# Up-projection blocks all from rounded parts in a ring of four, with the rounding of the score maxima on another engine

## The chip, the cores and the metric

The kernel runs on one core of a Trainium2 chip. The metric is the device time of one execution in microseconds. A core has TensorE (matrix products), VectorE, ScalarE and GpSimd, which run their own streams of instructions in order, and SyncE, which issues DMA transfers. They meet through semaphores.

## The reference

Eight batches of 512 rows with 256 columns pass through two attentions and a mixture of experts. Cut to what matters here:

```python
x = L0_attn_query                                   # (8, 512, 256)
x = x + _layernorm(attn(_layernorm(x)))             # 16 heads, rope, window of 250
# the second part, ffn(src) with src = _layernorm(x):
x = _rmsnorm(src + full_attention(src) @ Wo, norm1_w)
shared = _swiglu(flat @ W_shared_in) @ W_shared_out     # 256 -> 2 x 512 -> 256
h = _swiglu(flat @ W1_shared)                           # 256 -> 2 x 512, for all experts
routed = sum(h @ W2_experts[e] * w[:, e:e + 1] for e in range(8))   # w: two of eight are not zero
out = _rmsnorm(x + shared + routed, norm2_w)
```

## The kernel before

The matrices are tiled to 128 partitions. A batch i is worked on in two bodies, each of them heads (projection, rotation, transposes to the stacks q_t and k_t), then `attention(i, f, e, a)` with a = 0 for the windowed attention and a = 1 for the full one. Beside the first body the previous batch f = i - 1 does its up projection; beside the second body, and beside the heads, its expert outputs; the last of these run in the batch after that (e).

`attention` is a loop over steps m from -28 (LEAD) to 63. At step m TensorE makes the max score unit m + 28 (line 750), VectorE takes its maximum (1229 or 1232), and for m >= 0 TensorE makes the score unit m (777), whose exponentials ScalarE takes (630), GpSimd masks (505, 509) and TensorE weighs (791). Four groups of 16 steps (UNITS) cover 16 heads. Steps below 0 are called the lead here, the others the quiet steps. When the 16 maxima of a group are there, `split_max` rounds them into a high and a low part in m_split (VectorE, 1243 and 1244); TensorE transposes them (`max_rows`, 759, two units later), ScalarE copies the rows, and SyncE places them in q_t by small DMAs (`place_maxima`, 352). The score units of the group wait for those.

The up projection has 2 * NH = 8 blocks of hidden columns, each with a gated half and another half, and two input chunks: 32 products a batch. `HIDDEN_AT` gives the step of each: 16 in the lead, 16 at QUIET, steps 2, 5, 9 and 13 of each group. Blocks 0 to 3 (W_shared_in) multiply rounded parts: high and low weights times high and low rows, three matmuls a product (line 826, weights wup_r, rows xn_hi and xn_lo, which live in the stack buffers). Blocks 4 to 7 (W1_shared) are plain float32 matmuls (line 830, weights wup_s, kept in SBUF), of which each shows as two records. The rounded weights come from DRAM (wup_parts) through wup_r, a ring of RING = 2 blocks, by `load_up` on SyncE. They are made once, by GpSimd in batch 0 (`split_up`), and so are the expert pairs (`split_pair`).

VectorE follows each block with two operations (`gated_half` 1408, `hidden` 1415), two steps after the product that they need. In the last batch the up projection runs alone in `last_hidden`, with six banks in turn, and VectorE does STEPS_AT_LAST = 9 steps of other work (gates, the finish of the batch before) after each block.

Between the transposes of the second source xn and the product after them TensorE runs `unread(st[1], 2)` (line 879), two matmuls that nothing reads, while ScalarE copies the transposed rows. Their results are not used.

What sets the order: each engine's program is written out by hand in these tables of steps, and each runs in order.

## Time and profile before

| | us |
|---|---|
| three runs | 1986.41, 1979.39, 1984.70 |
| median | 1984.7 |
| the profiled execution's own time | 1978.52 |
| its span, first to last instruction | 1976.8 |
| TensorE busy | 1833.7 (93%) |
| VectorE busy | 1345.6 (68%) |
| ScalarE busy | 807.6 (41%) |
| GpSimd busy | 382.1 (19%) |

A busy share says how long an engine had work, over all stages; it doesn't say which engine a stage waits for. Matmuls overlap in the profile, so that a busy TensorE can still have waited a little. In the rows below, PE is TensorE, DVE is VectorE, ACT is ScalarE, POOL is GpSimd, and PEclk is the granted TensorE clock as a share of 2.4 GHz.

### The profile page before, as it was taken

The page shows a single profiled execution, that of the slowest core. Times are in us where ns is not written, and L with a number is a line of the kernel's source. Part 1 is how long each engine was busy: PE and PEld are TensorE (multiplying, and loading weights), DVE is VectorE, ACT ScalarE, POOL GpSimd, SP SyncE. Part 2 cuts the span into 40 slices and gives each one's busy share as a digit, 9 for nine tenths or more (in the row PEclk, how much of TensorE's full clock was granted, in tenths as well). Part 3 has the DMA queues.
Part 4 walks back from the last instruction along what each step waited for, and adds up shares of the span by engine and source line. Part 5 has one row for each costly group of instructions (what it writes and reads, how often), then busy time and mean ns, then how long its engine had stood idle before and what let it go on. Part 6 is the DMA issues. An engine that isn't in the chain of part 4 may idle for free.

```text
span 1976.8 us, 27875 instructions
## 1 busy us (share of the span) xinstructions
PE 1833.7 (93%) x9216; PEld 1022.6 (52%) x9216; DVE 1345.6 (68%) x4116; ACT 807.6 (41%) x1730; POOL 382.1 (19%) x671
## 2 busy tenths in 40 slices
PE   7968899989999999999999999998999999999988
PEld 4343464636555364644637355463645537364466
DVE  6457474775768668685876857677586856868466
ACT  3433535245343634335353353425534363443510
POOL 2336024101231013200251011410123101320010
PEclk8585999999999999999999999899999999999999
DMA  3026002201031100401022010220103110040240
GB/s 110 2 84 236 23 22 87 86 2 54 23 139 44 44 22 13 163 20 48 29 97 87 2 54 23 97 85 2 54 23 139 44 44 23 26 157 1 97 170 11
DMA packets 31295, 123.04 MB, mean 62 GB/s; under 512 B 5424, under 2 KB 18352, under 8 KB 26544
## 3 DMA queue, kind: packets, MB, share of 16 engines
q1 hardware_dynamic: 28624, 105.54, 14.9%
q0 software_dynamic: 2528, 15.73, 2.1%
q8 instruction: 73, 1.20, 0.2%
q14 instruction: 70, 0.57, 0.1%
HBM read 101.33 MB, written 18.87 MB: 61 GB/s over the span
## 4 chain that ended last, share of the span: by engine, by line
PE 74%; DVE 17%; issue 5%; ACT 3%; DMA 1%; POOL 0%; SPq 0%; DVEq 0%; ACTq 0%; POOLq 0%
PE fb L852 12%; PE ot L791 10%; PE sm L750 8%; PE fb L830 6%; DVE negmax L1232 6%; PE st L777 5%; PE fb L826 4%; PE st L718 3%; PE dn L718 3%; PE fb L848 3%; PE st L734 3%; DVE sm L1229 2%; DVE acc L1430 2%; PE sm L777 2%; PE ot L718 2%
## 5 line engine op out<-in xcount | busy, mean ns | idle before, releaser
L630 ACT ACTIVATE probs<-st 128x512 f32<-128x512 f32 (+3 forms) x832 | 395.4, 507 | 388.1 <-PE st L777 384.4
L852 PE MATMUL fb<-w_r,h_r 128*128 128x512 f32 x1344 | 391.5, 418 | 0.0
L750 PE MATMUL sm<-k_t,q_t 48*128 48x512 f32 (+3 forms) x864 | 313.8, 447 | 63.8 <-DVE negmax L1229 31.1
L1232 DVE TENSOR_REDUCE negmax<-sm 128x1 f32<-128x512 f32 x416 | 268.8, 685 | 83.5 <-PE sm L750 83.4
L777 PE MATMUL st<-q_t,k_t 64*128 64x512 f32 (+3 forms) x832 | 298.7, 453 | 22.3 <-ACT probs L630 19.9
L750 PEld LDWEIGHTS sm<-k_t,q_t 48*128 48x128 f32 x864 | 144.5, 195 | 315.3 <-DVE negmax L1229 136.5
L852 PEld LDWEIGHTS fb<-w_r,h_r 128*128 128x128 f32 x1344 | 231.0, 189 | 92.3 <-issue 56.3
L1229 DVE CUSTOM_DVE_ANT_0 sm<-sm,mask_qk 128x384 f32<-128x384 f32 (+1 forms) x448 | 202.1, 469 | 94.6 <-PE sm L750 91.5
L791 PE MATMUL ot<-probs,v_s 128*32 128x512 f32 (+3 forms) x2048 | 252.7, 536 | 2.9 <-POOL probs L505 2.9
L464 POOL TENSOR_TENSOR stack<-rot,stack 128x256 fp32r<-128x256 f32 x64 | 50.0, 782 | 980.7 <-ACT stack L566 980.7
L777 PEld LDWEIGHTS st<-q_t,k_t 64*128 64x128 f32 x832 | 133.6, 193 | 122.4 <-ACT probs L630 88.0
L505 POOL TENSOR_SCALAR_AFFINE_SELECT probs<-probs 128x256 f32<-128x256 f32 x256 | 105.6, 413 | 374.2 <-ACT probs L630 373.6
L1430 DVE SCALAR_TENSOR_TENSOR acc<-fb,gate,acc 128x256 f32<-128x256 f32 x224 | 107.8, 481 | 79.8 <-PE fb L852 74.5
L830 PE MATMUL fb<-xn_t,wup_s 128*128 128x512 f32 x232 | 130.2, 646 | 0.0
L826 PE MATMUL fb<-stack,wup_r 128*128 128x512 f32 x348 | 110.4, 434 | 1.4 <-DMA wup_r<-wup_parts 1.4
L630 ACT ACTIVATE probs<-sm 128x512 f32<-128x512 f32 (+2 forms) x192 | 85.6, 501 | 39.5 <-PE sm L777 39.2
L791 PEld LDWEIGHTS ot<-probs,v_s 128*32 128x32 f32 x2048 | 51.6, 110 | 78.2 <-issue 41.5
L566 ACT ACTIVATE stack<-rot 128x512 fp32r<-128x512 f32 x128 | 73.7, 624 | 43.1 <-DVE rot L1213 42.2
L734 PE MATMUL st<-ident_r,stack 128*128 128x128 f32 x704 | 85.1, 256 | 5.3 <-DVE q_t L1218 3.6
L1249 DVE RECIPROCAL den<-dn 128x16 f32<-128x16 f32 x64 | 16.2, 254 | 106.5 <-PE dn L803 106.3
L566 ACT ACTIVATE xn_t<-dn 128x512 f32<-128x512 f32 x40 | 23.9, 598 | 158.0 <-PE dn L713 158.0
L734 PEld LDWEIGHTS st<-ident_r,stack 128*128 128x128 f32 x704 | 69.1, 141 | 21.2 <-issue 8.9
(214 smaller groups left out, 2589.9 us busy)
## 6 DMA issues: line engine op xcount, KB each, us to landing
w_r<-w_parts SPq DMA_DIRECT2D x30, 2048.0 KB, 8.0
wup_r<-wup_parts SPq DMA_DIRECT2D x32, 512.0 KB, 4.0
w_parts<-w_r POOLq DMA_DIRECT2D x4, 2048.0 KB, 9.4
x_s<-in_L_attn_query SPq DMA_DIRECT2D x8, 512.0 KB, 4.7
q_t<-rot_b SPq DMA_DIRECT2D x256, 4.0 KB
x_kept<-o_s SPq DMA_DIRECT2D x8, 512.0 KB, 3.0
h_s<-in_L_ffn_W_experts POOLq DMA_DIRECT2D x8, 512.0 KB, 5.3
xa<-x_kept SPq DMA_DIRECT2D x8, 512.0 KB, 3.3
```

The lines of the kernel that those rows point to most:

```text
L630: nc.scalar.activation(probs[:, n % PSLOTS, 0:hi - lo], score_bank(m)[:, 0:hi - lo], ACT.Exp, scale=float(D) ** -0.5).then_inc(s_ex, 1)
L718: last = mm(dst, src_t[:, c, t * P:(t + 1) * P], w[:, c, :], start=(c == 0), stop=(c == NC - 1))
L734: last = nc.tensor.transpose(stack_bank(a, t, k)[:, b * P:(b + 1) * P].bitcast(F32R), stack[:, t % 2, pr:pr + 2, :].rearrange("p h s -> p ...
L750: mm(max_bank(w, a)[:, 0:hi - lo], q_t[r:r + MROW, b, t * P:(t + 1) * P], k_t[r:r + MROW, b, lo:hi], start=True, stop=True).then_inc(s_sm, 1)
L777: mm(score_bank(w)[:, 0:hi - lo], k_t[r:r + SK, b, j * P:(j + 1) * P], q_t[r:r + SK, b, lo:hi], start=True, stop=True).then_inc(s_st, 1)
L791: last = mm(ot[VW * c:VW * (c + 1), lo:hi], v_s[:, j, g * GH + c, :], probs[:, n % PSLOTS, 0:hi - lo], start=(j == 0), stop=(j == NT - 1), ...
L826: product = mm(bank[:, :], wup_r[:, n % RING, w, half, c, :], (xn_hi, xn_lo)[x][:, c], start=(c == 0 and k == 0), stop=(c == NC - 1 and k ...
L830: product = mm(bank[:, :], wup_s[:, c, col:col + P], xn_t[:, c, :], start=(c == 0), stop=(c == NC - 1))
L852: last = mm(fb[q % 2][:, :], h_r[:, h, m, rows], w2_r[:, k % 2, w, m, :], start=(m == 0 and n == 0), stop=(m == NH - 1 and n == 2))
L1229: return v.tensor_tensor_reduce(scores, scores, mask_qk[:, BACK * P - (hi - lo):BACK * P], -1.0, -MASKED, ALU.add, ALU.min, negmax[:, g % ...
L1232: return v.tensor_reduce(negmax[:, g % 2, n // GH, c:c + 1], max_bank(g * UNITS + n, a)[:, 0:hi - lo], AX.X, ALU.max, negate=True).then_in ...
L1430: add = v.scalar_tensor_tensor(acc[:, t, :], fb[q % 2][:, (e % 2) * E:(e % 2 + 1) * E], gate[:, t, e:e + 1], acc[:, t, :], ALU.mult, ALU.add)
```

## The change

1. Blocks 4 to 7 take the path of blocks 0 to 3: their weights are split into rounded parts too (a second `split_up`, before the expert pairs), stored in wup_parts, and loaded block by block. wup_s and its load are gone. Each product is now three matmuls on rounded parts (line 845 of the changed kernel).
2. RING is 4. In a batch SyncE loads four blocks after the residual and blocks 4 and 5, 6, 7 between the groups of `place_maxima`.
3. QUIET has five steps a group (2, 4, 6, 9, 13), so the lead has 12 products. QUIET_OUT starts at step 3 in every group, and the slices of expert outputs in the second body's lead end a step earlier.
4. For all batches but the first, `split_max` runs on GpSimd. VectorE gets a wait for it before the first maximum of groups 2 and 3.
5. The `unread` after the transposes of xn becomes slice 0 of expert output 7, which stood in the heads of the second body.
6. STEPS_AT_LAST is 9, 9, 4, 4, 4, 4 for the blocks of the last batch, and 9 beside the shared outputs as before.

```diff
-QUIET = [g * UNITS + n for g in range(NGR) for n in (2, 5, 9, 13)]
-QUIET_OUT = [g * UNITS + n for g in range(NGR) for n in ((2, 8, 12) if g else (3, 8, 12))]
+QUIET = [g * UNITS + n for g in range(NGR) for n in (2, 4, 6, 9, 13)]
+QUIET_OUT = [g * UNITS + n for g in range(NGR) for n in (3, 8, 12)]
...
-OUT_AT = [-LEAD] + spread(len(OUT_BESIDE) * NH - len(QUIET_OUT) - 1, 1 - LEAD, 1) + QUIET_OUT
+OUT_AT = [-LEAD] + spread(len(OUT_BESIDE) * NH - len(QUIET_OUT) - 1, 1 - LEAD, 0) + QUIET_OUT
-RING = 2
-STEPS_AT_LAST, STEPS_BESIDE_LAST = 9, 9
+RING = 4
+STEPS_AT_LAST, STEPS_BESIDE_LAST = (9, 9, 4, 4, 4, 4), 9
...
# SyncE, place_maxima, after the four DMAs of group g
+                    if f is not None:
+                        for n in ((4, 5), (6,), (7,), ())[g]:
+                            load_up(f, n)
...
# SyncE, load_up
-                if n >= RING:
+                if n >= RING or not isinstance(f, int) or f > 0:
                     sp.wait_ge(s_ub, f * N_UB + n - RING + 1)
-                elif f > 0:
-                    sp.wait_ge(s_ub, (f - 1) * N_UB + NH - RING + n + 1)
...
# GpSimd
+            def split_max(i, a, gr):
+
+                count = (i - 1) * N_MS + a * NGR + gr + 1
+                pool.wait_ge(s_mx, i * N_MX + (a * NGR + gr + 1) * UNITS)
+                if gr >= 2:
+                    pool.wait_ge(s_mp, i * N_MP + a * NGR + gr - 1)
+                m = negmax[:, gr % 2].rearrange("p t (b h) -> p h b t", b=2)
+                hi = m_split[:, gr % 2, :, 0]
+                lo = m_split[:, gr % 2, :, 1]
+                g.tensor_copy(hi, m).then_inc(s_mh, 1)
+                pool.wait_ge(s_mh, count)
+                g.tensor_tensor(lo, m, hi.bitcast(F32), ALU.subtract).then_inc(s_ms, 1)
...
+                    if f is not None and m % UNITS == 2 and m // UNITS + 1 < NGR:
+                        split_max(i, 0, m // UNITS + 1)
...
# TensorE, after the transposes of xn
-                    unread(st[1], 2)
+                    expert_out(f, 7, 0)
...
# VectorE, attention
-                        take_max(i, a, *divmod(m + LEAD, UNITS))
+                        gr, n = divmod(m + LEAD, UNITS)
+                        if f is not None and gr >= 2 and n == 0:
+
+                            dve.wait_ge(s_ms, i * N_MS + a * NGR + gr - 1)
+                        take_max(i, a, gr, n)
...
-                    if (m + LEAD) % UNITS == UNITS - 1 and m + LEAD < ALL:
+                    if f is None and (m + LEAD) % UNITS == UNITS - 1 and m + LEAD < ALL:
                         split_max(i, a, (m + LEAD) // UNITS)
```

TensorE in the first quiet group, steps 2 to 6, before. L830 is a plain up product, L750 a max score unit, L777 a score unit, L759 the transpose of the maxima:

```order
L830 MATMUL fb<-xn_t,wup_s 128x512
L750 MATMUL sm<-k_t,q_t 128x384
L777 MATMUL st<-q_t,k_t 128x384
L750 MATMUL sm<-k_t,q_t 128x128
L777 MATMUL st<-q_t,k_t 128x384
L750 MATMUL sm<-k_t,q_t 128x128
L777 MATMUL st<-q_t,k_t 128x384
L830 MATMUL fb<-xn_t,wup_s 128x512
L750 MATMUL sm<-k_t,q_t 128x128
L777 MATMUL st<-q_t,k_t 128x384
L759 MATMUL dn<-ident,m_split 32x128
```

And with the change, from the same product on (L845 is the product, L774 the max unit, L801 the score unit, L783 the transpose):

```order
L845 MATMUL fb<-stack,wup_r 128x512 x3
L774 MATMUL sm<-k_t,q_t 128x384
L801 MATMUL st<-q_t,k_t 128x384
L774 MATMUL sm<-k_t,q_t 128x128
L801 MATMUL st<-q_t,k_t 128x384
L845 MATMUL fb<-stack,wup_r 128x512 x3
L774 MATMUL sm<-k_t,q_t 128x128
L801 MATMUL st<-q_t,k_t 128x384
L774 MATMUL sm<-k_t,q_t 128x128
L801 MATMUL st<-q_t,k_t 128x384
L783 MATMUL dn<-ident,m_split 32x128
L845 MATMUL fb<-stack,wup_r 128x512 x3
```

The product that followed step 5's units now stands after step 4's, and one more stands after the transpose in step 6.

GpSimd at the start of the first body's masks of batch 1, before (L537 makes the low rows, L505 and L509 mask):

```order
L537 TENSOR_TENSOR stack<-xn_t,stack 128x32x16 [waits expert_rows_high_made,stack_transposes_done]
L537 TENSOR_TENSOR stack<-xn_t,stack 128x32x16 [waits expert_rows_high_made]
L505 AFFINE_SELECT probs<-probs 128x2x128 [waits exps_done]
L509 AFFINE_SELECT probs<-probs 128x2x134
L505 AFFINE_SELECT probs<-probs 128x2x128 [waits exps_done]
L509 AFFINE_SELECT probs<-probs 128x2x134
```

And with the change (L556 makes the low rows, L502 and L504 round the maxima, L515 and L519 mask):

```order
L556 TENSOR_TENSOR stack<-xn_t,stack 128x32x16 [waits expert_rows_high_made,stack_transposes_done]
L556 TENSOR_TENSOR stack<-xn_t,stack 128x32x16 [waits expert_rows_high_made]
L502 CAST m_split<-negmax 128x2x8 [waits max_taken]
L504 TENSOR_TENSOR m_split<-negmax,m_split 128x2x8 [waits max_high_made_by_pool]
L515 AFFINE_SELECT probs<-probs 128x2x128 [waits exps_done]
L519 AFFINE_SELECT probs<-probs 128x2x134
L515 AFFINE_SELECT probs<-probs 128x2x128 [waits exps_done]
L519 AFFINE_SELECT probs<-probs 128x2x134
L502 CAST m_split<-negmax 128x2x8 [waits max_taken]
L504 TENSOR_TENSOR m_split<-negmax,m_split 128x2x8 [waits max_high_made_by_pool]
```

The rounding of group 0 stands ahead of the first mask, that of group 1 behind the masks of steps 0 to 3.

## Rows read from the trace of the kernel before

**Rows 1.** Windows: us; PE, PEld, DVE, ACT, POOL busy; PEclk; DMA share; GB/s.
```profile
936.40:1044.70 108.30, 103.83 (x557) 58.24 (x556) 81.84 (x302) 47.33 (x114) 35.79 (x70) 1.00 0.17 60
1044.70:1168.80 124.10, 117.38 (x591) 64.41 (x590) 84.34 (x208) 52.78 (x101) 6.17 (x8) 1.00 0.15 52
1168.80:1282.80 114.00, 109.63 (x557) 60.10 (x556) 81.87 (x302) 47.42 (x114) 35.76 (x70) 0.94 0.16 57
...
972.00:977.00 5.00, 5.00 (x26) 3.39 (x25) 4.06 (x15) 0.60 (x1) 0.00 (x0) 1.00 0.27 103
```
**Rows 2.** Chain of waits, end of the first body's lead: start us, us, what.
```profile
981.29 0.21 DVE st L1229
...
987.10 0.44 PE sm L750
```
**Rows 3.** Chain of waits: up products of both kinds in the first body.
```profile
971.29 0.93 PE fb L826 x3
...
972.93 1.67 PE fb L826 x6
...
987.54 1.06 PE fb L830 x2
...
1031.61 0.86 PE fb L830 x2
```
**Rows 4.** Timelines of PE and DVE: start, us, instruction, idle before and releaser.
```profile
989.84 0.32 PE L750 MATMUL sm<-k_t,q_t 48*128 48x128 f32 x1 [0.69 <-DVE negmax L1229]
...
989.82 0.32 DVE L1243 CAST m_split<-negmax 128x16 fp32r<-128x16 f32 x1
...
990.42 0.15 DVE L1384 TENSOR_TENSOR gprob<-gprob,esum 128x4 f32<-128x4 f32 x1
...
1108.49 0.50 PE L750 MATMUL sm<-k_t,q_t 48*128 48x512 f32 x1 [1.43 <-DVE negmax L1232]
```
**Rows 5.** Chain of waits through the second body's heads and lead.
```profile
1059.07 0.86 PE st L879 x4
...
1064.98 3.00 PE fb L852 x12
...
1088.73 4.79 DVE negmax L1232 x8
...
1093.86 0.49 DVE acc L1430
```
**Rows 6.** GpSimd's small operations (timeline), and all casts of the maxima (min/median/max ns).
```profile
57.20 0.20 POOL L509 TENSOR_SCALAR_AFFINE_SELECT probs<-probs 128x12 f32<-128x12 f32 x1
...
132.18 0.72 POOL L464 TENSOR_TENSOR stack<-rot,stack 128x256 fp32r<-128x256 f32 x1 [22.93 <-ACT stack L566]
...
L1243 DVE CAST m_split<-negmax x64: 174/176/980, 41.8 to 1841.8; 128x16 fp32r<-128x16 f32 x64
```
**Rows 7.** Tail: one block on the chain, then the timeline of TensorE.
```profile
1882.69 3.02 PE st L826 x12
...
1891.87 3.17 PE L826 MATMUL fb<-stack,wup_r 128*128 128x512 f32 x12 [1.45 <-DMA wup_r<-wup_parts]
...
1908.10 3.60 PE L830 MATMUL sm<-xn_t,wup_s 128*128 128x512 f32 x8
1915.24 8.86 PE L848 MATMUL fb<-wso_s,h_s 128*128 128x256 f32 x32 [3.55 <-DVE sg L1451]
```
**Rows 8.** GpSimd in batch 0: low parts of the up weights, and its last store.
```profile
103.47 4.66 POOL L526 TENSOR_TENSOR h_r<-h_s,h_r 128x1024 fp32r<-128x1024 f32 x2
...
186.09 0.59 POOL L489 DMA_DIRECT2D w_parts<-w_r  x1 [0.30 <-POOL w_r L485]
```
**Rows 9.** From the page: a hidden operation of VectorE, and the loads of the ring.
```profile
L1415 DVE SCALAR_TENSOR_TENSOR sg<-sg,fb 128x512 f32<-128x512 f32 x28 | 19.2, 686 | 20.6 <-PE fb L830 20.2
...
wup_r<-wup_parts SPq DMA_DIRECT2D x32, 512.0 KB, 4.0
```
**Rows 10.** Window in the quiet steps of batch 5, columns as in rows 1.
```profile
1230.00:1245.00 15.00, 13.84 (x59) 5.42 (x59) 8.77 (x36) 6.42 (x16) 5.33 (x12) 0.61 0.01 3
```

More of the change, by code:

```diff
@@ L227, in build @@
         s_ms, N_MS = sem("max_split"), 2 * NGR
+        s_mh = sem("max_high_made_by_pool")
         s_mp, N_MP = sem("max_transposed"), 2 * NGR
@@ L269, in build @@
         s_wup = sem("up_weights_stored")
-        s_wu, N_WU = [sem(f"up_weights_loaded{k}") for k in range(RING)], 16 * NH // RING
-        wup_parts = nc.dram_tensor("wup_parts", (NH, P, 2, 2, NC, P), F32, kind="Internal").ap()
+        s_wu, N_WU = [sem(f"up_weights_loaded{k}") for k in range(RING)], 16 * 2 * NH // RING
+        wup_parts = nc.dram_tensor("wup_parts", (2 * NH, P, 2, 2, NC, P), F32, kind="Internal").ap()
         w2_parts = nc.dram_tensor("w2_parts", (PAIRS, P, 2, NH, 2 * E), F32, kind="Internal").ap()
@@ L386, in batch @@
                     x1_from_dram(e)
-                if f is not None:
-                    for n in range(RING, NH):
-                        load_up(f, n)
-                place_maxima(i, 0)
+                place_maxima(i, 0, f)
                 if f is not None:
@@ L409, in _ @@
             batch(0, None, None, True)
-            sp.wait_ge(s_wup, 16)
+            sp.wait_ge(s_wup, 32)
             for n in range(RING):
@@ L420, in _ @@
             load_pair(B - 1, 1, B - 2)
-            for n in range(RING, NH):
+            for n in range(RING, 2 * NH):
                 load_up(B - 1, n)
@@ L515, in mask_probs, with load_up_raw, split_up @@
                                 hidden_low(f, k)
-            def split_up():
-                pool.wait_ge(s_wur, 16)
+            def load_up_raw(u):
+                if u > 0:
+                    pool.wait_ge(s_wul, NC * u)
+                g.dma_start(wup_raw, (w_si, w1)[u].rearrange("(c p) n -> p c n", p=P)).then_inc(s_wur, 16)
+            def split_up(u):
+                pool.wait_ge(s_wur, 16 * (u + 1))
+                if u > 0:
+                    pool.wait_ge(s_wup, 16 * u)
                 for c in range(NC):
@@ L539, in rows_low @@
                                     ALU.subtract).then_inc(s_xl, 1)
-            g.dma_start(wup_raw, w_si.rearrange("(c p) n -> p c n", p=P)).then_inc(s_wur, 16)
+            load_up_raw(0)
             low_parts(0, 0)
             mask_probs(0, None)
-            split_up()
+            split_up(0)
+            load_up_raw(1)
             low_parts(0, 1)
+            split_up(1)
             load_raw(0)
@@ L555, in _ @@
                 rows_low(i - 1, i * N_SP + 16)
+                split_max(i, 0, 0)
                 mask_probs(i, i - 1)
                 low_parts(i, 1)
+                for gr in range(NGR):
+                    split_max(i, 1, gr)
             rows_low(B - 1, B * N_SP)
@@ L817, in hidden @@
                     pe.wait_ge(s_xl, f * N_XL + c + 1)
-                if n < NH and s % 4 == 0:
+                if s % 4 == 0:
                     pe.wait_ge(s_wu[n % RING], f * N_WU + 16 * (n // RING + 1))
-                up_product(fb[half], f, n, half, c)
-            def up_product(bank, f, n, half, c):
-                if n < NH:
-                    for k, (w, x) in enumerate(((0, 0), (0, 1), (1, 0))):
-                        product = mm(bank[:, :], wup_r[:, n % RING, w, half, c, :], (xn_hi, xn_lo)[x][:, c],
-                                     start=(c == 0 and k == 0), stop=(c == NC - 1 and k == 2))
-                else:
-                    col = half * HID + (n - NH) * P
-                    product = mm(bank[:, :], wup_s[:, c, col:col + P], xn_t[:, c, :], start=(c == 0), stop=(c == NC - 1))
+                for k, (w, x) in enumerate(((0, 0), (0, 1), (1, 0))):
+                    product = mm(fb[half][:, :], wup_r[:, n % RING, w, half, c, :], (xn_hi, xn_lo)[x][:, c],
+                                 start=(c == 0 and k == 0), stop=(c == NC - 1 and k == 2))
                 if c == NC - 1:
@@ L1046, in last_hidden @@
                             pe.wait_ge(s_xl, f * N_XL + c + 1)
-                        if half == 0 and c == 0 and n < NH:
+                        if half == 0 and c == 0:
                             pe.wait_ge(s_wu[n % RING], f * N_WU + 16 * (n // RING + 1))
-                        up_product(hidden_banks[n % 3][half], f, n, half, c)
+                        for k, (w, x) in enumerate(((0, 0), (0, 1), (1, 0))):
+                            product = mm(hidden_banks[n % 3][half][:, :], wup_r[:, n % RING, w, half, c, :],
+                                         (xn_hi, xn_lo)[x][:, c], start=(c == 0 and k == 0), stop=(c == NC - 1 and k == 2))
+                    product.then_inc((s_up, s_ub)[half], 1)
             def last_expert_out(t, k):
@@ L1611, in _ @@
                 if n < 2 * NH - 2:
-                    for _ in range(STEPS_AT_LAST):
+                    for _ in range(STEPS_AT_LAST[n]):
                         next(others, None)
@@ L1615, in _ @@
                 last_shared_out(q)
-                for _ in range(STEPS_AT_LAST):
+                for _ in range(STEPS_AT_LAST[0]):
                     next(others, None)
```

16 lines of the change are left out of this document (7 added, 9 removed).

## The prediction

> **What bounds the kernel now.** I read the busy time by stage first [rows 1]. A batch repeats every 232.4 us in two bodies, the first attention (936.4 to 1044.7) and the second (1044.7 to 1168.8). TensorE is busy for 103.8 of 108.3 us and for 117.4 of 124.1 us; VectorE for 81.8 and 84.3. TensorE is the bound on average, but it idles 4.5 + 6.7 us a batch, and the reader should look for those. Then the chain of waits [rows 2]: up to 981.2 it is one unbroken run on TensorE, and from there to the end of the lead (987.1) it hops between VectorE and TensorE. So the lead has a TensorE part and a VectorE part. Among the quiet steps TensorE stands 0.69 us before the sixth step of a group (step 5, counted from 0), waiting for a maximum [rows 4]. In the second body the lead's chain is nearly all maxima on VectorE [rows 5]. The last batch's tail is a third stage, with its own waits [rows 7].
>
> **Dearer or cheaper products.** A first-half product of the up projection is three single-pass matmuls: 1.67 us for two, 0.83 each (0.93 where it starts after a maximum). A second-half product is two records of 1.06 us together, 0.86 at the least [rows 3]. The change makes all 16 second-half products of a batch of the first kind. Price: 16 x (1.06 - 0.93) = 2.1 us of TensorE work less a batch; the ends are no gain (0.86 against 0.83) and 16 x 0.23 = 3.7. The Trainium skill ("FP8 and Floating Point Precision", TensorE Precision Notes) says true FP32 takes four passes of the array. By that rule, as an estimate, four passes against three would save a quarter of the time; the rows show an eighth to a fifth, so the rows decide.
>
> **The lead of the first body.** It drops from 16 to 12 products. Before step -10, where the chain is TensorE's, ten become seven: 3 x 0.93 = 2.8 us. After it the chain is VectorE's, 5.9 us [rows 2]; one operation of 0.69 of the up projection's [rows 9] leaves it. That makes 3.5 at best. But VectorE is already busy for 4.06 of 5.0 us at 972 to 977 [rows 1], so squeezing TensorE makes the maxima late sooner. Walking the steps with 0.93 a product, 0.3 to 0.66 a maximum and 0.68 a gated step, I get the end of the lead 2.4 us earlier. Ends: 1.2 and 3.5.
>
> **The quiet steps of the first body.** 16 products become 20. TensorE work: 4 x 0.93 more, 16 x 0.13 less, so +1.6 us. Against it stands idle time that the new places fill: the product that stood at step 5 is now at step 4 and another at 6, so the 0.69 us wait before the maximum of step 5 [rows 4] is covered in groups 0 and 1, and about 0.4 of a like wait in group 2: -1.8. The hidden product of VectorE at the end of group 0 moves to step 11, out of a stretch that VectorE bounds: up to -0.6, of which I take half. At the end GpSimd gets a 1.4 us subtraction at step 58 instead of 52, ahead of the last two masks; TensorE already waits there for a mask: +0.3. Sum +1.6 - 1.8 - 0.3 + 0.3 = -0.2. First body: -2.4 - 0.2, and I shave it to **-2.2** for waits that I can't see; ends -0.5 and -3.5.
>
> **The maxima's rounding moves from VectorE to GpSimd.** Eight pairs of small operations a batch. In the quiet stage the cast starts at 989.82 and VectorE's next work at 990.42, 0.65 us with the gap ahead; in the second body VectorE ends its maxima at 1093.52 (1088.73 + 4.79) and goes on at 1093.86; back-to-back operations overlap by about 0.1, which makes 0.43 us [rows 4, 5]. In the first body three of them sit beside the waits counted above, and I count nothing more. In the second body two lie on the chain: at 1093.6 (chain all VectorE) and at 1106.5, behind which TensorE stands 1.43 us [rows 4]. 2 x 0.43 = 0.9; a third (1122.7) may give 0.3: **-1.2**, ends 0 and -1.7. What is new is a wait of TensorE's transpose of the maxima for GpSimd, and everything on TensorE is queued behind it. No row shows this operation on GpSimd. Nearest rows: 0.20 us for 128x12 and 0.72 for 128x256 [rows 6]; I take 0.2 each, 0.5 for the pair with its semaphore. The transpose comes two maxima after the last of its group, at least 0.9 us later; in the quiet steps three steps, over 3 us. It is hidden; uncovered it costs its excess over that. GpSimd is in order: its masks wait behind the pair by no more than 0.5 us and were 8 slots ahead. VectorE's new wait (group two's first maximum on the pair of two groups before) is met a group earlier.
>
> GpSimd's operations and VectorE's can hold each other up: the cast of a maximum takes 174 ns at best, 335 among the masks, 980 at the worst [rows 6]. The Trainium skill ("SBUF — State Buffer", Who interferes with whom) calls the shared port pair an exclusive lock, where the loser blocks for the whole instruction; the trace agrees in direction. It speaks against more small work on GpSimd. By the rows the price is at most 16 pairs of 0.2 us, and what VectorE's own casts paid among the masks (0.65 against 0.43) goes. I count zero.
>
> **The filler.** Between the transposes of the second source and its projection TensorE runs a filler of 0.86 us, then later a group of 12 matmuls in 3.0 us that VectorE's next rotation waits behind [rows 5]. Now three of those 12 (0.75) stand in the filler's place. They need one output read by VectorE, which starts right after the second source is ready (TensorE's transposes of it start at 0.9 us before the filler) and takes 1.0 us, so the bank is free within 0.2 us of TensorE getting there (1059.07). The filler's time goes, the later group shrinks: **-0.8**; ends 0 and -0.9. The second body's three quiet slices move by one step: zero, ends +0.5 and -1.5. Second body: **-2.0**, ends +0.5 and -3.5 (-1 likely at least).
>
> **The ring and the loads.** 1 MB a batch becomes 2 MB after the residual and 2 MB inside the first body, 0.5 MB at a time at 4.0 us each [rows 9]; it used to be 1 MB and 1 MB. SyncE issues blocks 4 and 5 behind the score rows of group 0 (step -9), needed at 13 and 25; blocks 6 and 7 at 7 and 23, needed at 38 and 52. A step is 0.8 us, so each has 12 us or more. DMA is busy for 17% of the stage [rows 1]. Hidden; uncovered, 4 us each. In the start GpSimd gets about 8 us more (4.66 for the low parts, 2 for the high ones, gaps and an issue) before the expert weights; they are done at 186 and now near 195, an estimate,, needed only in batch 1 [rows 8]. Zero, ends -3 and +3.
>
> **The tail.** Before, TensorE waits 1.45 us for block 2 until 1891.87, runs two blocks of 3.02 and four of 3.43 (1908.10 is the last one's start: 2 x 3.02 + 3 x 3.43 = 16.3), and then waits 3.55 us for VectorE until 1915.24 [rows 7]. The ring holds four blocks already; block 4's load takes the place of block 2's and lands by 1891.7, five us before its use. So block 2 starts at 1890.4 and six blocks of 3.02 end at 1908.5. VectorE now does four side steps a block, not nine, 1.3 + 1.7 us against 3.0; its last product adds 0.75: 1909.3. **-5.9**; ends -4 and -6.5. The 19 side steps left over run beside the shared outputs, 8.9 us of TensorE.
>
> **The sum.** Seven batches have this work: 7 x (2.2 + 2.0) = 29.4, and 5.9: 35.3 us. The profiled execution took 1978.5 us (span 1976.8) and is the shortest of those shown; the median is 1984.7. I subtract from the median: **1949 us**. From the profile it would be 1943. The difference may be the clock: in this execution TensorE fell from 2.4 to 1.2 GHz once, in batch 5 (0.61 of it granted at 1230 to 1245), in steps with waits for VectorE, and that body took 114.0 instead of 108.3 us [rows 1, 10]. The medians may hold more such falls.
>
> **Rivals.**
> A, VectorE takes over: the lead gives 1.2, the quiet steps cost 0.7, the second body gives 1.0. 7 x 1.5 + 5.9 = 16.4: 1968. For it: VectorE has little room after 976. Chance 0.17.
> B, the clock: denser quiet steps remove the fall, and all parts come near their upper ends: 7 x 6 + 6 + 5.7 = 54: 1931. Chance 0.13.
> C, the other way with the clock: the fall comes in every batch, since steps 14 to 17 are as empty as before. 6 x 5.7 = 34 us takes all of it: 1983, no change. Against it: six of seven batches have none. Also here: the ring hides nothing that cost time and the products save nothing. Chance 0.10.
> D, slower: GpSimd hands the rounded maxima over late, and TensorE stands before the transpose in each first-body group. Behind a mask (0.8) and a held-up subtraction (1.4) that is 2.2 us beyond its slack, three times in seven batches, 46 us: 1985 + 46 - 35 = 1996. It decides from the point where the pair ends later than step 6 of a group. Against it: over 3 us of slack. Chance 0.05.
>
> **How the numbers follow.** The forecast (1935 to 1965) has 0.55. A measurement tells 0.5% from no change, that is 1975 to 1995. Faster by more: the forecast, A and B, 0.85. Same: C, 0.10. Slower: D, 0.05. The range 1928 to 1972 takes in the forecast, A's and most of B's times, and leaves out about 0.2.
>
> **What would show it.** The batch period near 228 us; TensorE busy 3 us a batch less; the first body near 106, the second near 122; no wait over 0.3 us at step 5; no release of the transpose by GpSimd; no wait for up blocks; the shared outputs starting 38 us after the last attention's end, not 43.6. A period above 231, or the transpose waiting for GpSimd, would make the prediction wrong.

## The result, and the profile after

The changed kernel took **1998.2 us** (median of six runs, 1990.5 to 2028.6) against 1985.0 us for the kernel before on the same chip (six runs, 1973.4 to 1990.0). The ratio is 1.0059, with a 95% interval of 1.0033 to 1.0085: 0.6% slower, where 1949 us and faster was forecast. (The run of 2028.6 us, over 1.5% above the fastest, is left out of the ratio.) The profiled execution took 2001.8 us (span 2000.0) at a mean granted clock of 0.940; that of before took 1978.5 us (span 1976.8) at 0.962.

I cut both spans at the end of the last exponential of each attention. A first body is then its heads, its lead and its quiet steps, all counted from the end of the second body before it. The columns of the window rows are those of [rows 1]; the last three are the granted clock, the DMA share and GB/s. First the changed kernel: batch 0, the seven first bodies in order, and the tail.

```profile
0.00:231.70 231.70, 186.11 (x798) 91.51 (x798) 128.84 (x380) 95.29 (x204) 90.38 (x125) 0.68 0.31 111
231.70:343.50 111.80, 105.25 (x574) 62.99 (x570) 65.68 (x246) 46.96 (x113) 33.27 (x75) 0.97 0.16 58
467.70:582.30 114.60, 109.65 (x572) 65.17 (x566) 79.69 (x293) 46.92 (x113) 34.99 (x75) 0.93 0.18 65
706.60:821.30 114.70, 109.75 (x572) 65.16 (x566) 79.94 (x293) 46.96 (x113) 35.05 (x75) 0.93 0.18 65
945.50:1060.60 115.10, 109.67 (x572) 65.09 (x566) 80.00 (x293) 47.05 (x114) 35.05 (x75) 0.93 0.17 65
1184.80:1292.80 108.00, 102.73 (x572) 60.69 (x566) 79.60 (x293) 46.98 (x114) 35.03 (x75) 1.00 0.19 69
1417.00:1529.10 112.10, 107.01 (x572) 63.30 (x566) 79.86 (x293) 46.99 (x114) 35.05 (x75) 0.95 0.18 67
1653.20:1768.00 114.80, 109.83 (x572) 64.73 (x566) 80.02 (x293) 46.96 (x114) 34.98 (x75) 0.93 0.17 65
1892.20:2000.00 107.80, 96.13 (x428) 75.98 (x422) 68.76 (x234) 11.07 (x22) 7.65 (x6) 0.97 0.30 115
```

The same cuts in the kernel before: batch 0, an ordinary first body, the one with the fall of the clock that [rows 10] showed, and the tail.

```profile
0.00:226.30 226.30, 178.27 (x798) 86.75 (x798) 129.69 (x380) 95.07 (x204) 82.21 (x119) 0.72 0.27 99
462.30:570.80 108.50, 104.35 (x558) 58.17 (x554) 81.63 (x301) 46.72 (x114) 34.11 (x68) 1.00 0.15 55
1159.60:1273.40 113.80, 110.14 (x558) 60.01 (x554) 81.62 (x301) 46.78 (x114) 34.11 (x68) 0.94 0.15 52
1862.50:1976.80 114.30, 99.79 (x412) 74.11 (x406) 70.57 (x234) 11.37 (x21) 7.62 (x6) 0.97 0.26 99
```

Between the two spans lie 23.2 us. Batch 0 gave +5.4, the seven first bodies +24.6 (791.1 against 766.5), the seven second bodies -0.3 (869.5 against 869.8), the tail -6.5. So nearly all of the loss is in the first bodies, and six of seven there have a granted clock below 1. (In five of them, batches 2 to 4, 6 and 7, a fall begins in the lead, 41.7 to 44.7 us into the body; in batch 1 it begins at the lead's end and lies in the quiet steps.) One, from 1184.8, has full clock throughout and takes 108.0 us, 0.4 less than before. That row is the important one: **two things went wrong, not one.** The clock cost some 33 us (the six others against 108.0, of batch 1's against 110, since it took 110.6 before with full clock; an estimate from these rows), and even with full clock the change brings next to nothing outside the tail.

Cut finer, with the lead's end at the first exponential. First the stretches of an undisturbed batch of before (heads and lead, then quiet steps; first body, then second).

```profile
927.20:985.70 58.50, 58.19 (x289) 39.69 (x284) 41.86 (x145) 18.00 (x36) 9.41 (x10) 1.00 0.08 28
985.70:1035.60 49.90, 46.16 (x270) 18.45 (x272) 39.66 (x157) 28.66 (x78) 24.70 (x58) 1.00 0.23 84
1035.60:1103.70 68.10, 65.73 (x322) 44.05 (x316) 49.97 (x125) 16.86 (x34) 7.84 (x10) 1.00 0.20 72
1103.70:1159.60 55.90, 51.13 (x275) 20.45 (x276) 34.70 (x86) 36.59 (x70) 0.00 (x0) 1.00 0.11 39
```

And the changed kernel: a lead with the fall, then the undisturbed batch.

```profile
706.60:770.60 64.00, 62.21 (x277) 42.11 (x272) 41.33 (x146) 17.56 (x35) 9.84 (x12) 0.87 0.07 25
...
1184.80:1242.00 57.20, 55.09 (x277) 37.50 (x271) 40.89 (x145) 17.50 (x35) 9.83 (x12) 1.00 0.08 28
1242.00:1292.80 50.80, 47.65 (x296) 23.19 (x296) 38.71 (x151) 29.48 (x79) 25.20 (x63) 1.00 0.31 116
1292.80:1360.30 67.50, 64.86 (x317) 43.49 (x314) 49.47 (x122) 16.87 (x33) 9.02 (x14) 1.00 0.22 79
1360.30:1417.00 56.70, 50.99 (x275) 20.25 (x278) 34.13 (x81) 36.83 (x70) 1.28 (x6) 1.00 0.11 39
```

At full clock the lead gives 1.3 us, the quiet steps cost 0.9, the second body's lead gives 0.6 and its quiet steps cost 0.8. With the fall the first stretch takes 64.0 us where it takes 57.2. Where does the fall lie? Here are two stretches of the body that starts at 706.6.

```profile
743.30:748.30 5.00, 4.49 (x19) 2.52 (x18) 3.41 (x16) 0.60 (x1) 2.20 (x2) 1.00 0.00 0
748.30:753.30 5.00, 4.83 (x13) 3.23 (x14) 2.62 (x10) 0.00 (x0) 0.00 (x0) 0.50 0.01 3
```

The clock is at 0.50 (1.2 GHz) from 748.3 to 765.4. The timeline of TensorE at its start shows what stood there (start, duration, operation, and in brackets the idle time before it with what ended it).

```profile
746.77 0.65 PE L845 MATMUL fb<-stack,wup_r 128*128 128x512 f32 x2
747.36 0.44 PE L774 MATMUL sm<-k_t,q_t 48*128 48x256 f32 x2
748.47 0.68 PE L774 MATMUL sm<-k_t,q_t 48*128 48x384 f32 x1 [0.68 <-DVE negmax L1248]
749.08 1.02 PE L742 MATMUL dn<-wgate_s,xn_t 128*128 128x10 f32 x4
749.96 1.63 PE L845 MATMUL fb<-stack,wup_r 128*128 128x512 f32 x3
```

L845 is the up product (826 and 830 before), L774 the product for a maximum. TensorE waits 0.68 us for VectorE's maximum, and within this wait the clock goes down; a product then takes 1.63 us instead of the 0.93 of [rows 3]. Ahead of it stand stack transposes of 128 columns, products with 48 rows and with 10 columns, and a few full products. The undisturbed body has the same 0.68 us wait at the same place, so the wait alone does not bring the fall. The Trainium skill ("TensorE: Matmul & The Clock Gate", HAM oscillation) ties such falls to stretches without matmuls. The rows go further than the page: here the longest pause just before the fall was 0.68 us, and TensorE was busy for 4.49 of the last 5.0 us.

The waits of TensorE in the undisturbed first body (us in total, times, longest):

```profile
PE sm L774 <- DVE negmax L1248: 2.4, 6, 0.8
PE ot L815 <- POOL probs L515: 1.2, 2, 0.7
PE dn L783 <- POOL m_split L504: 1.0, 1, 1.0
```

The second of the two waits for masks, at step 50:

```profile
1283.03 0.41 PE L815 MATMUL ot<-probs,v_s 128*32 128x128 f32 x4 [0.74 <-POOL probs L515]
```

The waits for maxima were 3.3 us a batch before, all in the quiet steps, as in [rows 4]. Two thirds of what is left of them stands in the lead now, and two kinds are new: the weighing (L815) waits for GpSimd's masks, and the transpose of the maxima (L783) for GpSimd's rounding. In the second body's quiet steps one wait is new too:

```profile
1408.35 0.66 PE L827 MATMUL dn<-ident,o_t 128*128 128x128 f32 x4 [0.94 <-ACT o_t L590]
1408.76 0.95 PE L868 MATMUL fb<-w_r,h_r 128*128 128x512 f32 x3
```

TensorE waits 0.94 us for ScalarE's copy of the outputs before it transposes them. In the kernel before, the same two stood the other way round, and the slice of an expert output covered ScalarE:

```profile
1150.02 0.96 PE L852 MATMUL fb<-w_r,h_r 128*128 128x512 f32 x3
1151.03 0.66 PE L803 MATMUL dn<-ident,o_t 128*128 128x128 f32 x4
```

The tail did what was forecast. Where [rows 7] had six blocks with side steps and a 3.55 us wait until 1915.24, 52.7 us after the last exponential, the shared outputs now start 46.4 us after it:

```profile
1928.77 3.10 PE L1066 MATMUL fb<-stack,wup_r 128*128 128x512 f32 x12
...
1938.57 2.64 PE L864 MATMUL fb<-wso_s,h_s 128*128 128x256 f32 x11 [0.85 <-DVE sg L1474]
```

### The profile page after: what moved, and what is told of

It reads as the page before. It is cut to its first block, busy times and chain, and to the rows that moved or that the text cites. A ratio compares the mean times of both kernels' runs of the same rounds, so it can differ in the third digit from the quotient of the medians.

```text
span 2000.0 us, 28159 instructions
## 1 busy us (share of the span) xinstructions
PE 1847.0 (92%) x9316; PEld 1061.1 (53%) x9316; DVE 1323.3 (66%) x4004; ACT 811.2 (41%) x1730; POOL 413.6 (21%) x789
## 4 chain that ended last, share of the span: by engine, by line
PE 71%; DVE 15%; issue 6%; ACT 4%; POOL 2%; DMA 1%; SPq 0%; ACTq 0%; DVEq 0%; POOLq 0%
PE fb L868 12%; PE ot L815 10%; PE fb L845 8%; PE sm L774 8%; DVE negmax L1251 6%; PE st L801 4%; PE dn L742 3%; PE st L742 3%; PE st L758 3%; PE fb L864 3%; DVE acc L1453 2%; PE ot L742 2%; PE dn L827 2%; ACT probs L654 2%; PE sm L801 1%
## 5 line engine op out<-in xcount | busy, mean ns | idle before, releaser
L774 PE MATMUL sm<-k_t,q_t 48*128 48x512 f32 (+3 forms) x864 | 313.3, 455 | 49.6 <-DVE negmax L1248 24.0
L801 PE MATMUL st<-q_t,k_t 64*128 64x512 f32 (+3 forms) x832 | 297.4, 456 | 21.7 <-ACT probs L654 19.9
L774 PEld LDWEIGHTS sm<-k_t,q_t 48*128 48x128 f32 x864 | 143.3, 198 | 272.9 <-DVE negmax L1248 115.3
L868 PEld LDWEIGHTS fb<-w_r,h_r 128*128 128x128 f32 x1344 | 230.1, 188 | 85.6 <-issue 49.9
L815 PE MATMUL ot<-probs,v_s 128*32 128x512 f32 (+3 forms) x2048 | 258.2, 538 | 13.8 <-POOL probs L515 13.8
L845 PE MATMUL fb<-stack,wup_r 128*128 128x512 f32 x672 | 244.3, 476 | 0.0
L801 PEld LDWEIGHTS st<-q_t,k_t 64*128 64x128 f32 x832 | 131.4, 193 | 126.2 <-ACT probs L654 90.1
L515 POOL TENSOR_SCALAR_AFFINE_SELECT probs<-probs 128x256 f32<-128x256 f32 x256 | 108.8, 427 | 306.1 <-ACT probs L654 305.8
L1453 DVE SCALAR_TENSOR_TENSOR acc<-fb,gate,acc 128x256 f32<-128x256 f32 x224 | 107.8, 481 | 88.4 <-PE fb L868 83.1
L845 PEld LDWEIGHTS fb<-stack,wup_r 128*128 128x128 f32 x672 | 122.1, 210 | 42.1 <-issue 23.9
L502 POOL CAST m_split<-negmax 128x16 fp32r<-128x16 f32 x56 | 11.4, 204 | 486.6 <-DVE negmax L1251 403.1
L815 PEld LDWEIGHTS ot<-probs,v_s 128*32 128x32 f32 x2048 | 51.9, 110 | 96.6 <-issue 46.4
```

What stands on the lines that cost most here:

```text
L515: last = g.affine_select(out=late, in_=late, compare_op=ALU.is_ge, fill=0.0, base=0, pattern=[[0, 2], [1, P]], channel_multiplier=-1)
L774: mm(max_bank(w, a)[:, 0:hi - lo], q_t[r:r + MROW, b, t * P:(t + 1) * P], k_t[r:r + MROW, b, lo:hi], start=True, stop=True).then_inc(s_sm, 1)
L801: mm(score_bank(w)[:, 0:hi - lo], k_t[r:r + SK, b, j * P:(j + 1) * P], q_t[r:r + SK, b, lo:hi], start=True, stop=True).then_inc(s_st, 1)
L815: last = mm(ot[VW * c:VW * (c + 1), lo:hi], v_s[:, j, g * GH + c, :], probs[:, n % PSLOTS, 0:hi - lo], start=(j == 0), stop=(j == NT - 1), ...
L845: product = mm(fb[half][:, :], wup_r[:, n % RING, w, half, c, :], (xn_hi, xn_lo)[x][:, c], start=(c == 0 and k == 0), stop=(c == NC - 1 an ...
L868: last = mm(fb[q % 2][:, :], h_r[:, h, m, rows], w2_r[:, k % 2, w, m, :], start=(m == 0 and n == 0), stop=(m == NH - 1 and n == 2))
```

## The experiments

**Theories.** L: the lead of 12 products is too thin (TensorE has too little work in it), and that brings the fall of the clock near its end. G: GpSimd's late rounding makes holes that bring it. P: the cheaper products, of three matmuls on rounded parts, bring it.

**1. Four quiet steps in the changed kernel (q4).**

```
-QUIET = [g * UNITS + n for g in range(NGR) for n in (2, 4, 6, 9, 13)]
+QUIET = [g * UNITS + n for g in range(NGR) for n in (2, 5, 9, 13)]
```

> The changed kernel with four quiet steps a group (2, 5, 9, 13) in the first body, so 16 products in the lead as before; all else as changed. Theory L (the thinner lead): in the changed kernel the granted clock fell to 1.2 GHz in six of seven first bodies, at the end of a lead that has 12 products and more waits for VectorE. L expects at most one fall in seven bodies here, first bodies near 107 us (108.3 less about one for the cheaper products), a time of 1965 to 1977. Theory G (GpSimd's late rounding makes the holes) and theory P (the three-pass products themselves bring the fall) both expect that the falls stay: first bodies near 115, a time of 1993 to 2000.

It took 1979.3 us (ratio to before 0.999, 0.996 to 1.002). From batch 2 on no lead has a fall; it takes 58.4 to 58.6 us. But falls remain in the quiet steps: five of these six bodies have one or two, 3.4 to 27.3 us long, and they take 108.3 to 116.5 us. The sixth, without one:

```profile
1399.30:1457.70 58.40, 58.13 (x289) 39.73 (x284) 41.48 (x144) 18.00 (x36) 9.83 (x12) 1.00 0.08 28
1457.70:1506.40 48.70, 44.54 (x286) 21.47 (x288) 38.59 (x151) 28.74 (x78) 26.08 (x64) 1.00 0.30 108
```

So L holds for the lead, and five steps were a loss against four even without the clock: 48.7 + 58.4 = 107.1 against 108.0. TensorE's wait for GpSimd's rounding shrinks from 1.0 to 0.3 us in the undisturbed body, and the two waits of its quiet steps for masks are gone, so these too came from the fifth step. L's "at most one fall" was wrong, and with it its 1965 to 1977 us.

**2. The first body's rounding back on VectorE (s1).**

```
-                        if f is not None and gr >= 2 and n == 0:
+                        if f is not None and a == 1 and gr >= 2 and n == 0:
...
-                    if f is None and (m + LEAD) % UNITS == UNITS - 1 and m + LEAD < ALL:
+                    if (f is None or a == 0) and (m + LEAD) % UNITS == UNITS - 1 and m + LEAD < ALL:
```

(GpSimd's calls of `split_max(i, 0, ...)` are taken out.)

> The changed kernel with the rounding of the maxima of the first body back on VectorE (that of the second body stays on GpSimd). Theory G: the waits of TensorE for GpSimd at the transpose and at the weighing (2.9 us a batch in the changed kernel's undisturbed body) go, and with these holes the falls of the clock: first bodies near 106, a time of 1950 to 1965. Theories L and P: the falls stay in most bodies; the waits for GpSimd shrink by 1 to 2 us a batch, VectorE has 0.4 us more in three places: first bodies near 114, a time of 1985 to 1996.

It took 2012.0 us (ratio 1.014, 1.009 to 1.019). The falls stay in all six leads from batch 2 on, the quiet steps take 50.3 us where they have full clock (50.7 in the changed kernel), and the waits of the weighing for masks stay at 1.2 us a batch. G falls. It ran slower than the changed kernel, in each of its four executions (2002.9 to 2014.3 us). In the profiled one that goes with six disturbed leads against five and with a clock below 1 in the quiet steps of five of the seven bodies; why there are more isn't shown.

**3. Only the rounded up blocks, the ring and the tail (prod).** This is the kernel before with these three.

```
-RING = 2
+RING = 4
...
-STEPS_AT_LAST, STEPS_BESIDE_LAST = 9, 9
+STEPS_AT_LAST, STEPS_BESIDE_LAST = (9, 9, 4, 4, 4, 4), 9
...
+                for k, (w, x) in enumerate(((0, 0), (0, 1), (1, 0))):
+                    product = mm(fb[half][:, :], wup_r[:, n % RING, w, half, c, :], (xn_hi, xn_lo)[x][:, c],
+                                 start=(c == 0 and k == 0), stop=(c == NC - 1 and k == 2))
```

> The kernel before with the rounded up blocks in a ring of four, its load places, and the tail with nine and then four side steps, and nothing else: four quiet steps, filler, rounding on VectorE as before. Theory P: three-pass products bring the falls, first bodies near 114 and a time of 1990 or more. Theories L and G: at most one fall; 16 products at 0.13 us less are 2 us a batch where TensorE is the bound, and 6 to 7 us of tail: 1963 to 1975. If the products' price is hidden, 1978.

It took 1978.7 us (ratio 0.997, 0.995 to 1.000). The tail takes 107.8 us, the same 6.5 less as in the changed kernel. The leads stay at 58.5. The quiet steps of a first body tell more:

```profile
769.70:819.50 49.80, 46.20 (x286) 22.65 (x288) 40.64 (x158) 28.70 (x78) 24.98 (x58) 0.97 0.29 107
```

The clock is 0.97 there, in each first body from batch 3 on: half of the clock for 3.4 us, some 20 us into the quiet steps, where the kernel before had 1.00 in six of seven bodies. (Batch 1 has a fall of 27.3 us in its quiet steps and batch 2 one of 6.8.) The cheaper products should have saved 2.1 us and the stage is 0.1 to 0.2 shorter than 49.9. No fall in the leads: P doesn't explain those. A weaker P would explain the dip; no run takes the products apart from their loads and the ring.

**4. Five quiet steps in the kernel before (b5).** The diff of experiment 1 the other way, in the kernel before.

> The kernel before with five quiet steps a group (2, 4, 6, 9, 13) and so 12 products in the lead, and nothing else. Theory L: the falls come in five or more of seven first bodies, first bodies near 114, a time of 2005 to 2020. Theories G and P: the falls stay away, and the time is 1980 to 1990.

It took 2032.4 us (ratio 1.026, 1.020 to 1.031), slower than anything that L gave. One first body, its lead and its quiet steps:

```profile
716.40:780.60 64.20, 62.22 (x277) 41.66 (x271) 41.79 (x148) 17.52 (x36) 9.40 (x10) 0.86 0.08 26
780.60:834.40 53.80, 51.66 (x280) 21.23 (x280) 40.67 (x153) 29.29 (x79) 23.16 (x57) 0.94 0.23 90
```

A long fall (13.7 to 27.3 us) begins in the lead in four of the six bodies from batch 2 on, one of 3.4 us in the fifth, and in the sixth the fall begins just before the lead ends; all that with nothing of GpSimd's rounding and none of the new products in the kernel. Where the clock is full the quiet steps take 51.9 to 52.0 us, 2.1 more than before, the lead gives 1.1, and the second body's lead takes 68.5 where it took 68.0. So this one edit costs 1.5 us a batch at full clock, and bodies with long falls take 5 to 9 us more. Its quiet steps have the two waits for masks too (1.1 us), with the rounding on VectorE. L is confirmed, and P and G are out as the cause of the falls in the lead.

**5. Fillers in the lead (fill).**

```
-                            gate_logits(f, LOGITS_AT.index(m), 1 if e is None else 0)
+                            gate_logits(f, LOGITS_AT.index(m), 2)
```

> The changed kernel with two 256-column fillers of TensorE (0.86 us a pair, results unread) at each of the four steps of the lead of the first body at which the gate's logits are made, 3.4 us of filling in all, about what the four products that left the lead took. Theory L (the lead is too thin, whatever fills it): the 17 us at 1.2 GHz near the end of the lead go in at least five of seven bodies; lead and heads stage of the first body come down from 63.9 to 58 or 59 us (57.2 undisturbed, plus what of the fillers VectorE doesn't cover); a time of 1970 to 1982. Rival: the fall is tied to the waits for VectorE's maxima in the lead or to GpSimd's small operations and stays: 1998 to 2012.

```profile
704.30:765.20 60.90, 58.79 (x293) 40.60 (x287) 41.12 (x146) 17.52 (x35) 9.81 (x12) 0.99 0.08 25
765.20:819.40 54.20, 51.13 (x298) 25.14 (x296) 38.75 (x148) 29.44 (x79) 25.16 (x63) 0.91 0.29 110
1180.90:1241.60 60.70, 58.59 (x293) 40.58 (x288) 40.90 (x145) 17.52 (x35) 9.81 (x12) 1.00 0.08 27
```

The long falls in the lead are gone: fillers whose results nobody reads do it, with the waits for maxima still there (1.7 us a batch). Batch 1 says the same of every kernel here: there `gate_logits` runs one such filler at each of these steps already (the `1 if e is None` of the line above), and the changed kernel, s1, b5 and qout have no fall over 3.4 us at that place in it. The time is 2003.1 us all the same, not the 1970 to 1982 of L (ratio 1.012, 1.007 to 1.017). The fillers' 3.4 us lie wholly on the path (60.7 against 57.2), so my 58 to 59 was wrong, and in four of seven bodies a fall of 3.4 to 10.2 us came later instead, almost wholly in the quiet steps (clock 0.91 to 0.97).

**6. The second body's quiet slices at their old steps (qout).**

```
-QUIET_OUT = [g * UNITS + n for g in range(NGR) for n in (3, 8, 12)]
+QUIET_OUT = [g * UNITS + n for g in range(NGR) for n in ((2, 8, 12) if g else (3, 8, 12))]
```

> The changed kernel with the quiet slices of the second body at their old steps (2, 8, 12 in groups one to three). In the changed kernel TensorE waits 0.94 us for ScalarE's copy of the outputs at step 50 of the second body, and this stage takes 56.8 us where it took 55.9. If the moved slices are the cause, the wait goes and the stage takes 55.0 to 55.9. If the rounding on GpSimd or the slice in the filler's place is the cause, it stays at 56.8.

```profile
1600.20:1656.20 56.00, 51.75 (x276) 20.60 (x278) 34.16 (x81) 36.76 (x70) 1.27 (x6) 1.00 0.11 39
```

The wait is gone and the stage is back at 55.9 to 56.0 us, in all seven batches. The moved slice cost 0.8 us a batch. (Its time is 2005.6 us from two runs, ratio 1.013, 1.007 to 1.020. The profiled one has falls in five leads from batch 2 on, as the changed kernel, but longer ones, up to 30.7 us; in the first bodies nothing was changed.)

**7. GpSimd's subtractions later (late).**

```
+LOW_AT = (30, 48, 62, 62)
...
-                            if min(HIDDEN_AT[4 * (NH + k) + 3] + HIGH_LAG, ALL - 1) // 2 * 2 == m:
+                            if LOW_AT[k] == m:
```

(The old expression gives 30, 44, 58 and 62.)

> The changed kernel with two of GpSimd's four 1.3 us subtractions for the rounded hidden blocks moved behind masks of which TensorE has no need at once (from step 44 to 48 and from 58 to 62). Theory: TensorE's waits of 0.74 us at the weighing of step 50 and of 0.80 us at the end of the first body come from these subtractions ahead of its masks. Then both go or fall under 0.35: the undisturbed quiet stage takes 49.9 to 50.2 us where it takes 50.7, and the second body's lead 67.0 where it takes 67.5. Rival: they come from the rounding of the maxima on GpSimd or from the masks' own 0.4 us each; then both stay.

```profile
527.30:577.20 49.90, 47.48 (x300) 23.42 (x300) 38.15 (x151) 29.35 (x79) 25.04 (x63) 1.00 0.30 111
577.20:644.00 66.80, 64.67 (x317) 43.30 (x311) 49.45 (x122) 16.84 (x33) 9.47 (x13) 1.00 0.23 86
```

These are the first body's quiet steps and the second body's lead, at full clock. TensorE's wait for a mask at step 50 is gone, and the one behind the end of the first body is down from 0.80 to 0.33: 0.9 us less in the quiet steps, 0.7 in the second body's lead. (One run, 1992.0 us, with long falls in three leads and falls of 3.4 us in two.) In the changed kernel GpSimd's row reads as follows; the mask that TensorE needs stands behind the 1.27 us subtraction.

```profile
1280.97 0.41 POOL L515 TENSOR_SCALAR_AFFINE_SELECT probs<-probs 128x256 f32<-128x256 f32 x1 [0.29 <-ACT probs L654]
1281.35 1.27 POOL L490 TENSOR_TENSOR h_r<-sg,h_r 128x512 fp32r<-128x512 f32 x1
1282.57 0.85 POOL L515 TENSOR_SCALAR_AFFINE_SELECT probs<-probs 128x256 f32<-128x256 f32 x2
```

**8. The kernel before a second time (again).**

> The kernel before, unchanged, a second time. Its first profile had one fall of the clock in seven first bodies (13.7 us long) and 226.3 us up to the end of batch 0. If falls are rare in it, there is again at most one, and the period stays at 232.4 us; the time up to the end of batch 0 shows how far that alone varies with the clock (the changed kernel took 231.7).

One run, 1978.3 us. Batch 0 took 224.7 us, and no first body from batch 2 on has a fall (108.4 to 108.5 each), but some second bodies do (128.3 us in batch 2). Batch 0 varies with the execution: the kernel before, this repetition and b5, which have one program for it, took 226.3, 224.7 and 232.8 us, and nine profiles with the changed kernel's batch 0 took 224.7 to 236.2, all at a granted clock of 0.65 to 0.72. So the 5.4 us of the startup needs no cause in the change; that it has none isn't shown.

**9. Covered and uncovered fillers among the quiet steps (keep).** To prod, two fillers of 0.43 us a group.

```
+KEEP_AT = (4, 12)
...
+                        if m >= 0 and m % UNITS in KEEP_AT:
+                            keep(f, *divmod(m, UNITS))
```

`keep` waits until the bank's last product is read and makes one unread product of 256 columns.

> The kernel before with rounded up blocks, ring of four and the shorter tail, as in run prod, and two fillers of 0.43 us in each group of the first body's quiet steps (after steps 4 and 12), where TensorE waits 0.35 to 0.70 us for a maximum. Theory P2 (the cheaper products thin out the quiet steps, and the clock takes the gain back in a dip of 3.4 to 6.8 us in each body): the dips go, the quiet stage takes 48.6 to 49.4 us where prod has 49.7, a time of 1968 to 1975. Rival: the products' saving is hidden behind VectorE's maxima anyway; the stage stays at 49.7 or grows with the fillers to 51: 1979 to 1990.

```profile
769.80:819.70 49.90, 48.50 (x302) 24.11 (x304) 39.49 (x157) 28.68 (x78) 24.86 (x58) 1.00 0.30 109
```

The dip is gone in five of the six bodies from batch 2 on, and TensorE's waits for maxima fell from 3.1 to 1.2 us a batch; but eight fillers cost about what they bring: the stage takes 49.9 us, not the 48.6 to 49.4 of P2, and the kernel 1983.0 us (ratio 1.001, 0.998 to 1.003).

**10 and 11. The repaired change (best, best2).** The changed kernel with four quiet steps (experiment 1), the old slices (6) and fillers: eight in best, and in best2 only the four that stand where TensorE waits anyway.

```
+KEEP_AT = (4, 20, 28, 36)
...
+                        if m in KEEP_AT:
+                            keep(f, *divmod(m, UNITS))
```

> The changed kernel with four quiet steps a group in the first body (16 products in the lead), the old quiet slices of the second body, and two fillers of 0.43 us in each group of the first body's quiet steps. If the clock and the moved slices are what took the gain: no fall over 3.4 us from batch 2 on, first bodies near 107.2, second bodies near 122.7, a time of 1955 to 1966. If GpSimd's rounding has a price of its own, or the fillers are not covered: first bodies near 109, 1970 to 1980.

> Run best with four fillers in the first body's quiet steps instead of eight, each (after steps 4, 20, 28, 36) where the trace of q4 has TensorE waiting 0.35 to 0.70 us for a maximum. If covered fillers are enough to hold the clock: quiet stage 48.8 to 49.2 us where best has 50.0 (period 230 against 231.2), no fall over 3.4 us from batch 2 on, a time of 1957 to 1965. If the clock wants the others too: falls as in q4 (up to 13.7 us in half of the bodies), 1970 to 1980.

best took 1968.5 us (ratio 0.993, 0.990 to 0.996), between the two ranges expected: no first body from batch 2 on has a fall, but its quiet steps take 50.0 us. **best2 took 1957.2 us: ratio 0.985, 0.981 to 0.990**, faster than both kernels. Its batch:

```profile
927.20:985.60 58.40, 58.03 (x289) 39.56 (x283) 41.55 (x143) 17.99 (x36) 9.83 (x12) 1.00 0.08 28
985.60:1034.10 48.50, 47.18 (x297) 22.87 (x296) 38.68 (x152) 28.71 (x78) 26.11 (x64) 1.00 0.30 110
1034.10:1100.90 66.80, 64.65 (x317) 43.30 (x309) 49.41 (x122) 16.80 (x32) 8.28 (x12) 1.00 0.25 88
1100.90:1156.90 56.00, 51.76 (x275) 20.54 (x278) 34.16 (x81) 36.83 (x70) 1.28 (x6) 1.00 0.11 39
```

A period of 229.7 us against 232.4, with full clock in all twelve bodies from batch 2 on. Four covered fillers hold the clock as well as eight do and leave the quiet steps 1.5 us shorter. Here at last the cheaper products can be seen: 48.4 us a stage where the kernel before has 49.9. The fillers don't make this gain, since the body of q4 with full clock and without them took 48.7; but no run puts fillers into the kernel before, so that the products alone make it is argued, not shown.

**12. best2 with the first body's rounding on VectorE (best2s).**

> Run best2 with the rounding of the first body's maxima back on VectorE (that of the second body stays on GpSimd). Theory S: in the first body GpSimd's rounding is worth nothing where VectorE has room, or costs its waits of the transpose (0.16 us a batch in best2): quiet stage within 0.3 us of 48.4, time 1952 to 1962. Rival: it takes 0.43 us off VectorE's chain in each of the three groups of the quiet stage, and they come back: quiet stage 49.2 to 49.7, time 1962 to 1968.

1959.9 us (ratio 0.987, 0.983 to 0.991), quiet steps 48.3 to 48.6 us, as in best2. The difference from best2 is within the noise: in the first body it does not matter which engine rounds the maxima.

## Why the prediction was wrong, point by point

Per batch, at full clock, in us (the whole run for the tail):

| step of the prediction | forecast | measured | where |
|---|---|---|---|
| lead of the first body | -2.4 | -1.3 | changed kernel, undisturbed body |
| quiet steps | -0.2 | +0.9 | the same |
| second body | -2.0 | +0.2 | the same |
| clock | none | +2 to +7 in six of seven first bodies | changed kernel; cause by b5, q4, fill |
| tail | -5.9 | -6.5 | changed kernel, prod |
| batch 0 | 0 | +5.4 | varies by 8 without the change |

**The clock** was the main failure: some 33 us of the changed kernel's time, where the sum had nothing. The forecast kept the fall of one body in seven out of the sum, and rival B even had the denser quiet steps remove it. I looked at where the one fall of before lay (quiet steps) and asked only what the change does there. The change takes four products out of the lead, and I counted that as pure gain. Rival C (a fall in every batch, 1983 us) was nearest, but placed it at steps 14 to 17 and let the other gains stand. The long falls began in the lead, but for batch 1's: b5 brings them into the kernel before by this edit alone, and q4 and fill take them out of the changed one's leads. Falls in the quiet steps, which q4 keeps and which are longer there than in prod, have no cause shown.

**The lead.** "Walking the steps ... 2.4 us earlier" failed on its own warning: new waits of 1.6 us for VectorE's maxima, two of them 0.68 and 0.81. The undisturbed body also shows what these waits leave: the measured 1.3 is near the lower end that I gave, 1.2.

**The quiet steps.** In the sum +1.6 - 1.8 - 0.3 + 0.3 the failed term is the last, "GpSimd gets a 1.4 us subtraction at step 58: +0.3". Moving such subtractions (late) gave back 0.9 in the quiet steps and 0.7 in the second body's lead, so it was 1.6. I had looked at the last one only; the one at step 44 also stood ahead of a mask that TensorE needed next. With both out of the way the stage takes 49.9 us, as before, where the other terms sum to -0.5; TensorE's wait of 1.0 us for the rounded maximum (below) is still in it.

**The cheaper products.** The 2.1 us was about right as work (0.13 apiece), but it is seen only where the clock stays up: prod shows 0.1 to 0.2, q4's one undisturbed body 1.2, best2 1.5 (with fillers that are covered). In prod a dip of 3.4 us at half clock went with them.

**The second body.** The lead's part was right where no other edit spoils it: 66.8 us in q4 and best2 against 68.0 is -1.2, as much as the 0.8 of the filler and the 0.43 of one rounding (no run takes the two apart). The other roundings (0.43 and 0.3) brought nothing: the wait of 1.43 us in [rows 4] became two of 0.47 and 0.27, yet with the old slices the quiet steps take 55.9 us as before; where the rest went isn't shown. The failed step is "The second body's three quiet slices move by one step: zero, ends +0.5": it was +0.8, since a slice had hidden ScalarE's copy of the outputs. And 0.7 came over from the first body, through GpSimd's late mask (late).

**GpSimd's rounding.** Rival D named the transpose as its place. It did wait, 1.0 to 1.4 us a batch from batch 2 on in the changed kernel, since the pair came behind two masks and took 0.8 us with its gap (my 0.5), and up to 0.3 with four quiet steps. So "hidden" was wrong by a microsecond, D's 46 us by far more. best2s shows that in the first body the move buys nothing.

**Signs.** Two of the prediction's own signs of being wrong came: a period above 231 us (108.0 + 124.2 = 232.2 even with full clock) and the transpose waiting for GpSimd.

**Right:** the tail (a little more than forecast), the loads (no wait for an up block; a load took 5.2 us in the middle instead of the 4.0 of [rows 9], and was hidden), and the place of the first body's old waits.

## What to carry to other kernels

Work that moves off one stretch of TensorE must be checked on the stretch that it leaves: here four full products fewer in a lead of small transposes, short products and waits of 0.7 us halved its clock for 10 to 27 us. Unread fillers at four steps where TensorE waited anyway cost nothing that the stage shows (48.4 us against 48.7) and went with full clock; in the lead, where TensorE didn't wait, they cost their whole time. So read the waits first and place fillers one by one. When slices of work are shifted by "only one step", look for the copy on another engine that the slice had been hiding.

## What the runs showed that I had not expected

- TensorE's clock fell to 1.2 GHz with TensorE busy for 4.49 of 5.0 us and no pause over 0.68 us; the same instructions in another batch of the same execution kept 2.4 GHz.
- Batch 0, at a granted clock of about 0.7, moves the whole by up to 11 us between profiles with the same startup (224.7 to 236.2 us), which is why experiments on this kernel are better read by stage at full clock than by their total.
- Filling the lead didn't free the body of falls: in fill, leads with full clock were followed by shorter falls in four of seven quiet stages.
